# One weight column per slot, extra-key loads in halves, a separate image for the first batch, and an earlier high half in the last

## What is computed

```python
def _cross_attention(q_in, kv_in, wq, bq, wk, bk, wv, bv, wo, bo, bias_k, bias_v):
    qh = (q_in @ wq + bq).reshape(b, q_len, H, K)          # b=8, q_len=112, H=16, K=128
    kh = (kv_in @ wk + bk).reshape(b, t, H, K)             # t=375
    vh = (kv_in @ wv + bv).reshape(b, t, H, K)
    kh = concatenate([kh, bias_k], axis=1)                 # 376 keys
    vh = concatenate([vh, bias_v], axis=1)
    weights = softmax(einsum('bqhk,bthk->bhqt', qh, kh) / sqrt(K), axis=-1)
    return einsum('bhqt,bthk->bqhk', weights, vh).reshape(b, q_len, H * K) @ wo + bo
```

## Time and profile before

| | us |
|---|---|
| median of 3 runs | 2304.0 |
| lowest and highest run | 2300.95, 2304.62 |
| the profiled execution, whole time | 2299.39 |
| the profiled execution, span from first to last instruction | 2297.5 |
| PE busy in that span | 2230.2 |
| granted TensorE clock, mean of the span | 0.99 |

### The profile page before, as it was taken

The page is one execution under the profiler, slowest core; times in us unless marked ns, Lnnn a source line. Parts: engine busy times, 40 slices in busy tenths (PEclk is TensorE's granted clock), DMA queues, the critical chain, the costliest instruction groups (busy, mean ns, idle before and its releaser), DMA issues.

```text
span 2297.5 us, 36229 instructions
## 1 busy us (share of the span) xinstructions
PE 2230.2 (97%) x12347; PEld 2021.1 (88%) x12347; DVE 1375.1 (60%) x3070; ACT 1121.9 (49%) x2282; POOL 650.5 (28%) x945
## 2 busy tenths in 40 slices
PE   7999999999999999999999999999999999999999
PEld 6777788888999999899888898999899899888888
DVE  6877774524666666666644526666566565644743
ACT  5777753344455455455444434555455455443421
POOL 2111055421232332232322312233233133223421
PEclk9999999999999999999999999999999999999999
DMA  5422136566888988978965557987988888764110
GB/s 191 144 90 104 58 104 199 171 232 193 285 255 276 283 260 262 299 249 272 296 179 167 189 177 238 291 268 249 286 276 262 286 276 263 246 198 140 54 56 32
DMA packets 325462, 480.03 MB, mean 209 GB/s; under 512 B 65566, under 2 KB 249778, under 8 KB 323234
## 3 DMA queue, kind: packets, MB, share of 16 engines
q1 hardware_dynamic: 325282, 477.73, 64.9%
HBM read 368.72 MB, written 108.92 MB: 208 GB/s over the span
## 4 chain that ended last, share of the span: by engine, by line
PE 80%; DMA 7%; DVE 5%; SPq 3%; issue 2%; ACT 2%; POOL 0%; ACTq 0%; DVEq 0%
PE ps_o L1875 7%; PE ps_o L1877 7%; PE ps_o L1876 7%; PE ps_v L1875 6%; PE ps_v L1877 6%; PE ps_v L1876 6%; PE ps_k L1875 5%; PE ps_k L1876 5%; PE ps_k L1877 5%; DMA turned_probabilities<-blocks 4%; PE ps_t L1876 4%; PE ps_t L1875 4%; PE ps_t L1877 4%; PE ps_s L1875 3%; PE ps_s L1877 3%; PE ps_s L1876 3%
## 5 line engine op out<-in xcount | busy, mean ns | idle before, releaser
L941 POOL TENSOR_TENSOR pt_lo<-pt_lo,pt_hi 128x512 fp32r<-128x512 f32 x186 | 247.4, 1356 | 191.8 <-ACT pt_hi L1213 183.1
L1248 ACT ACTIVATE prob<-ps_s,row_columns 128x376 f32<-128x376 f32 x256 | 147.1, 575 | 245.9 <-DVE row_columns L1643 244.0
L934 POOL CAST k_hi<-xk_hi 128x1 fp32r<-128x1 f32 x256 | 51.9, 203 | 703.8 <-PE ps_s L1877 703.8
L1661 DVE STREAM_TRANSPOSE blocks<-prob 128x384 f32<-128x384 f32 x248 | 143.4, 578 | 145.4 <-DMA turned_probabilities<-blocks 138.4
L1875 PE MATMUL ps_k<-cs_hi,w_a_hi 128*128 128x376 f32 x636 | 220.4, 347 | 0.0
L1876 PE MATMUL ps_k<-cs_lo,w_a_hi 128*128 128x376 f32 x636 | 215.6, 339 | 0.0
L1877 PE MATMUL ps_k<-cs_hi,w_a_lo 128*128 128x376 f32 x636 | 214.4, 337 | 0.0
L1643 DVE TENSOR_REDUCE row_columns<-ps_s 128x1 f32<-128x376 f32 x256 | 139.2, 544 | 119.4 <-PE ps_s L1877 118.9
L1531 DVE TENSOR_SCALAR prob<-prob,row_columns 128x375 f32<-128x375 f32 (+1 forms) x384 | 199.2, 519 | 4.5
L889 POOL TENSOR_TENSOR w_b_lo<-w_raw_b,w_b_hi 128x512 fp32r<-128x512 f32 x80 | 108.0, 1376 | 330.2 <-ACT w_b_hi L993 330.2
L1875 PE MATMUL ps_t<-cs_hi,w_a_hi 128*128 128x376 f32 x512 | 172.2, 336 | 5.6 <-DVE q L1524 5.6
(11 more groups left out here) (290 smaller groups left out, 6305.0 us busy)
## 6 DMA issues: line engine op xcount, KB each, us to landing
ckd<-context_by_key_halves SPq DMA_DIRECT2D x256, 384.0 KB, 5.5
cs_hi<-context_halves SPq DMA_DIRECT2D x64, 752.0 KB, 6.3
cs_lo<-context_halves SPq DMA_DIRECT2D x64, 752.0 KB, 7.9
turned_probabilities<-blocks SPq DMA_DIRECT2D x62, 768.0 KB, 5.2
pt_lo<-turned_probabilities SPq DMA_DIRECT2D x248, 192.0 KB, 3.8
w_raw_b<-in_blocks_b SPq DMA_DIRECT2D x104, 256.0 KB, 3.9
w_raw_a<-in_blocks_a SPq DMA_DIRECT2D x104, 256.0 KB, 4.9
q<-q_scratch SPq DMA_DIRECT2D x64, 256.0 KB, 4.7
```

What stands on the lines that cost most here:

```text
L934: pool.tensor_copy(k[t % 2][0][:, LK:KW], xk[0][:, ds(col, 1)])
L941: pool.tensor_tensor(lo, lo.bitcast(F32), hi, ALU.subtract).then_inc(t_lo, 1)
L1248: act.activation(prob[buf][:, 0:KW], ps_s[buf][:, 0:KW], ACT.Exp, bias=max_neg[:, buf:buf + 1], accum_out=prob_sum[:, buf:buf + 1]).then_i ...
L1661: dve.transpose(blocks[:].rearrange("p (s j t e) -> p t j s e", s=4, j=3, t=NT)[:, t], prob[buf][:, 0:BLOCKS * SQUARE].rearrange("p (j s e ...
```

## The change

Four edits. The weight columns of the next group are loaded one per slot: slot a's four in batch 3, slot b's four in batch 4. The extra key's probabilities are loaded in two halves of 512 KB, one in slot 3 of quarter 2 (for quarters 0 and 1) and one in slot 3 of quarter 3. The first batch of an attention writes its squares into the front of `extra` instead of `blocks`, so that batch 1's first transpose waits for no store. In the last batch ACT makes the high half of batch 6 ahead of `last_turned_hi` and `exp`.

```diff
-        self.fetches = isinstance(self.b, int) and self.b == 3 and att.layer and group > 0
+        self.fetches = {3: 0, 4: 1}.get(self.b) if isinstance(self.b, int) and att.layer and group > 0 else None
...
+        def image(place):
+            return extra[:, 0:BLOCKS * P] if place.head and place.parity == 0 else blocks[:]
...
                 def load_extra(place):
+                    first = place.quarter - 2
                     for i in range(2):
-                        sp.wait_ge(extra_out[i], 16 * place.pairs + 16)
-                    sp.sem_inc(sp_waited, 1)
+                        sp.wait_ge(extra_out[i], 16 * (place.pairs + first))
                     wait(sp, z_term, NT * place.quads)
                     sp.sem_inc(sp_waited, 1)
-                    src = pex_scr[ds(place.block, 1), ds(place.b - 3, 4)].rearrange("o b f -> o (b f)")
-                    sp.dma_start(extra[:, 0:4 * NT * P], src.partition_broadcast(P)).then_inc(extra_in, 16)
+                    src = pex_scr[ds(place.block, 1), ds(place.b - 2 + first, 2)].rearrange("o b f -> o (b f)")
+                    sp.dma_start(extra[:, 2 * first * NT * P:(2 * first + 2) * NT * P],
+                                 src.partition_broadcast(P)).then_inc(extra_in, 16)
...
-                    sp.dma_start(turned_scr[place.parity], blocks[:]).then_inc(blocks_out, 16)
+                    sp.dma_start(turned_scr[place.parity], image(place)).then_inc(blocks_out, 16)
...
-                            if place.quarter == 3:
+                            if place.quarter >= 2:
                                 load_extra(place)
...
-                        if t == 0 and place.fetches:
-                            load_block(0, place.block_a + 1)
-                        if t == 1 and place.fetches:
-                            load_block(1, place.block_b + 1)
+                        if place.fetches is not None:
+                            load_block(place.fetches, (place.block_a, place.block_b)[place.fetches] + 1, [t])
...
-                        act.wait_ge(extra_in, 16 * place.quads + 16)
+                        act.wait_ge(extra_in, 32 * place.quads + 32)
...
+                        if t == 0 and place.final:
+                            turned_hi(place.before())
                         if place.final and t < 2:
                             last_turned_hi(place, t)
                         if place.key(t + 2):
                             exp(*place.key(t + 2))
-                        if t == 0 and place.before():
+                        if t == 0 and place.before() and not place.final:
                             turned_hi(place.before())
...
-                        wait(dve, blocks_out, 16 * turned_batches(place))
-                    dve.transpose(blocks[:].rearrange("p (s j t e) -> p t j s e", s=4, j=3, t=NT)[:, t],
+                        wait(dve, blocks_out, 16 * (turned_batches(place) - (place.head and place.parity)))
+                    dve.transpose(image(place).rearrange("p (s j t e) -> p t j s e", s=4, j=3, t=NT)[:, t],
```

## The result

| us | before | changed | ratio, 95% interval |
|---|---|---|---|
| first comparison | 2302.5 (4 runs) | 2282.4 (4 runs, 2280.97 to 2284.63) | 0.9909, 0.9891 to 0.9926 |
| second comparison, in the last of the experiments | 2297.7 (10 runs) | 2273.8 (4 runs, 2272.16 to 2274.40) | 0.9897, 0.9882 to 0.9912 |

The changed kernel is faster by 20.0 us where 28.6 were forecast; the time, 2282.4 us, is inside the range of 2251 to 2288. The same kernel, measured again beside other runs of the kernel before, gained 23.9 us. Since times differ that much between comparisons, experiments are judged by the ratio to the runs of before that they were measured beside.

The account below looks back on a forecast made before the run. PE, busy 2230.2 of 2297.5 us, was taken to lose 39.2 us behind the fetch, where the DMA queue is full. Savings 17.0 + 2.6 + 9.0 = 28.6 us gave 2275 us, range 2251 to 2288.

Parts of the forecast that it names:

- Edit 1, forecast 17.0: Fetching groups, batches 3 and 4: path shorter by 2.55 us in each of six, 15.3, plus 1.7 of half clock.
- The signs named beforehand: Changed profile: DVE waits about 4 us at batch 3, 6 at batch 4; PE 0.5 to 1, head output 1.5 to 2.5.
- the half clock: One stretch at clock 0.93 behind the head output's wait: its 1.7 us were taken as gone.
- SP's issue time is no term: SP in slots 0 to 3: a column costs about 0.6 us to issue, with only a waiting store right behind it.
- Edit 2, forecast 0: Extra load in halves, 16 places: cost 0, bounds −0.1 to 0.3 us each; neutral in the weight columns' path.
- Edit 3, forecast 2.6: Batch 0 of each attention: first context sum ends 1.3 us earlier, 2.6 in all; bounds 0 and 8.5.
- The step in between: Batch 0's round trip is not faster: POOL still starts at 566.37 and needs 4.23 us for three thirds.
- Edit 4, forecast 9.0: Last batch of each attention: PE's products start 4.5 us earlier, twice 9.0; bounds 7 and 11.
- two waits named as late next: Last batch: PE waits for the last heads' probabilities, 0.3 us, and for `sums_lo` of the first sum, 0.7.
- B: Rival, chance 0.27: the DMA queue has room, so all 39.2 us behind the fetch go; 50.8 us saved, 2253 us.
- C: Rival, chance 0.13: stalls only move behind batch 4, with half clock, and eat the 17.0 us; 2292 us.
- D: Rival, chance 0.05: slower, batch 4's store landing some 13 us or more after its square; 2313 us at 10 a group.

Follow-up runs that it names:

- x6: Changed kernel with the weight columns moved to batches 1 and 5, two per slot in slots 2 and 3; 2250.0 us, ratio 0.9793.
- y1: The changed kernel itself, all four edits, measured again beside the last runs; 2273.8 us, ratio 0.9897.
- x1: Kernel before with only the weight columns loaded one per slot in batches 3 and 4; 2284.6 us, ratio 0.9937.
- y4: Changed kernel with the extra load whole again, 1024 KB in slot 3 of quarter 3; 2274.4 us, ratio 0.9898.
- y2: Changed kernel with both 512 KB halves issued one right behind the other in slot 3 of quarter 3; 2284.1 us, ratio 0.9936.
- x4: Kernel before with only batch 6's high half made ahead of the last batch's; 2290.9 us, ratio 0.9969.
- x2: Kernel before with only the extra load split in two halves; 2303.6 us, ratio 1.0019.
- x5: Changed kernel with the extra load whole again, 1024 KB, in an earlier session; 2275.8 us, ratio 0.9903.

## Why the prediction was right, and where its sizes were off

**The bound.** Read rightly: the path through the full queue, not the engines, made the fetching stretches long. x6 shows it by taking 37.7 us of the 40.9 us of steady excess away while the queue moves the same 477.73 MB.

**Edit 1, forecast 17.0, alone 14.5.** The mechanism came as described. Batch 3's late issue is gone, what is late next is batch 4's store, and the path is 2.35 us shorter where 2.55 was worked out (2.13 in y1, but only 1.30 in the changed kernel's first trace). Batch 4's store landed 7.9 to 9.3 us after its square there, where 9 was worked out. The signs named beforehand, in group 1: DVE's wait at batch 3 about 4 us, measured 4.50; at batch 4 about 6, measured 5.75; PE 0.5 to 1 us there, measured 0.57; 1.5 to 2.5 us at the head output, measured 1.67. Two things made the term too large. First, the half clock was taken as wholly gone (1.7 us), but x1 has three of six stretches at 0.93 or 0.94 in the batch behind. Secondly, "SP's issue time is no term" was wrong at batch 4: with the queue full SP is itself held up. One `ckd` issue took 3.87 us (above), and the same issue in the six groups took 2.98 to 5.29 us; at each of the six, eight earlier DMAs with 3552 KB had been issued and had not landed. And the mean delay from batch 4's last square to its store is 1.9 us in x1, 0.8 in the changed kernel, 0.1 before.

**Edit 2, forecast 0.** The sum in the changed kernel is 0 (y1 against y4, within what can be told), but for reasons that cancel, of which the prediction had one; that the term came true is in part luck. The dearer pair was in the bounds: 0.23 us a half, 0.46 a pair, measured 0.7. The Trainium skill (DMA: Bandwidth & Descriptors, Measured), which asks for transfers of at least 1 MiB, had given the prediction some 0.8 us a split by interpolation, an estimate. A straight line between the two sizes of its table, which was measured on transfers that GpSimd issued, gives 3.4 us a half and 0.6 us a split, again an estimate; y2 against y4, with 0.7 us, agrees with that better than with my reading of the rows. What neither gave is the gain from the place: a shorter queue ahead of the last `ckd`, and a delay in two parts instead of one. And the term held only beside edit 1; alone it costs 4.4 us.

**Edit 3, forecast 2.6.** Alone 1.8 us with an interval that includes 0; the traces show 36.80 + 35.77 → 34.50 + 35.47, which is 2.6, and 2.5 in the changed kernel. A single trace can't carry that alone, since the same two stretches are 1.6 us shorter in x4 and 0.3 us longer in x1, both without edit 3. Over all traces they come to 69.4 us in the mean of the ten kernels with edit 3 and 72.0 in the four without, which is 2.6 again; and no kernel with the edit has a score waiting for `k_lo` in batches 0 and 1, where the four without it have 2.1 to 3.7 us of such waits. The step in between was wrong: POOL did not still start at 566.37 but at 564.33, since the round trip of batch 0 does come earlier, and ACT's copy now waits 2.64 us for the reload. In the changed kernel's first trace nearly all of it came in attention 0 (2.2 of 2.5 us), not half in each.

**Edit 4, forecast 9.0.** Alone 7.1; its two stretches in the trace shorten by 3.5 us each. PE's wait for `pt_lo` fell to tenths as forecast (0.28 and 0.34). Of the two waits named as late next, that for `sums_lo` came, with 0.39 us where 0.7 was put; for the probabilities of the last heads PE waited nowhere in that batch. The half-clock stretch behind the gap is gone in x4 in both attentions. Not named was the `ckd` behind the `extra` load, 0.67 us in x4 and 1.9 us in y4 for both attentions. Edit 2 removes most of that (0.2 us left in y1), and these stretches gain 8.6 us in both traces of the changed kernel against 7.0 in x4 and 6.9 in y4.

**The sum.** Without edit 2, 14.5 + 1.8 + 7.1 = 23.4 us, which is what y4 measured (0.0102 × 2297.7 = 23.4) and, edit 2 being 0, nearly y1's 23.9. So the effects of edits 1, 3 and 4 add up within their intervals (each of some 2 to 3 us either way), and the forecast's 28.6 was 5 us too high by the steps above, 8.6 us against the first comparison. That the effects of the four single runs add to only 19.0 is x2's −4.4, which disappears when the columns no longer stand in front of the same store.

**What stays open.** The first comparison gave 20.0 us, the second 23.9, with intervals that overlap. The traces differ in the place: the steady excess is 37.5 us in the first and 27.1 in the second (28.7 to 28.8 in x1, x5 and y4, which have the same order of columns), with the path 0.8 us a group longer and one of six stretches at half clock instead of none. So the first trace stands alone, and no run says why the queue was slower there.

**The rivals.** B (the queue has room) is refuted: 1.03 of share and 25 to 32 us still lost. C (the stalls only move) has a part in it. In the first trace the batch 4 stretches lost 18.8 us of excess and the next ones took 12.0 of them back, so more of the term was eaten than kept; in y1 the two together fell from 39.2 to 25.1 us. D did not come: batch 4's store landed at most 9.3 us after its square, not 13.

## What to carry to other kernels

When one queue carries both bulk loads and a round trip that an engine waits for, count the bytes in front of each deadline, not the bytes in all: here the steady excess is 27 to 41 us with the eight columns in batch 3 or in batches 3 and 4, and 2 to 3 us with them in batches 1 and 5. Where a load is moved off a missed deadline, look which deadline comes next in the same queue, and whether another batch has nothing large in it. Effects on one such path don't add (edit 2 costs 4.4 us alone and nothing beside edit 1), while those of the edits on other paths did.

## What the runs showed of the hardware

- In a full queue (share 1.03) the issue itself can be held up: at one place of each of the six groups, with eight earlier DMAs not yet landed, a `ckd` issue took 2.98 to 5.29 us, where the median of all is 0.37, and everything behind it on SP waits. With three or fewer not yet landed, no issue in the attentions took over 1.8 us. Eight alone do not explain it, since the twelve other issues that found eight took under 1.6 us; what does is not shown.
- A 1024 KB load in two halves right behind each other takes 7.67 us instead of 6.95, and a 256 KB column occupies the queue for 1.0 us in the mean of 48, from landing to landing (median 0.9), where 0.85 was worked out from the mean rate.
- Not every idle gap is followed by the lower clock. Of the six head-output waits of the changed kernel, 1.36 to 2.15 us long, one was: this, in the row of the stretch 1788.34:1813.56 above.

```profile
1806.76 0.48 PE L1880 MATMUL ps_o<-sums_hi,w_b_hi 128*128 128x448 f32 x1 [2.15 <-DVE sums_lo L1677]
```
